# The learned message layer of a graph network: units transposed beforehand, tiles multiplied in pairs, all sums on TensorE

## The reference

```python
def _forward(x, edge_src, edge_dst, edge_vec, emb, norm, W1, W2):      # M = 8, MUL = 16, MOUT = 8
    xs = concat([x[edge_src, :8], x[edge_dst, :8]], axis=1)
    xv = concat([x[edge_src, 8:].reshape(E, 8, 3), x[edge_dst, 8:].reshape(E, 8, 3)], axis=1)
    h = 2.0 ** 0.5 * relu(emb @ W1 / 10.0 ** 0.5)                      # [E, 16]
    w = (h @ W2 / 16.0 ** 0.5).reshape(E, 7, MUL, MOUT)                # W2 is [16, 896]
    s_out = PW_S * (einsum('eu,euw->ew', xs, wa_s) + INV_SQRT3 * einsum('eui,ei,euw->ew', xv, y1, wb_s))
    g_out = PW_S * (einsum('eu,euw->ew', xs, wa_g) + INV_SQRT3 * einsum('eui,ei,euw->ew', xv, y1, wb_g))
    v_out = PW_V * (INV_SQRT3 * einsum('eu,ek,euw->ewk', xs, y1, wc) + INV_SQRT3 * einsum('eui,euw->ewi', xv, wd)
                    + einsum('eui,ea,iak,euw->ewk', xv, y2, W3J121, we))
    edge_ftr = concat([GAIN * tanh(s_out), (GAIN * tanh(g_out)[:, :, None] * v_out).reshape(E, 24)], axis=1) * norm
    return segment_sum(edge_ftr, edge_dst)
```

## Time and profile before

| | us |
|---|---|
| median of 3 runs | 16380.43 (16376.54 to 16397.94) |
| span of the profiled execution | 13418.0 |
| time of the profiled execution beside its span | not given by the page |
| PE busy | 6021.0 (45%) |
| PE weight loads busy | 5074.6 (38%) |
| DVE busy | 5448.5 (41%) |
| ACT busy | 2111.0 (16%) |
| POOL busy | 7502.6 (56%) |
| mean granted TensorE clock | 0.718 |

### The profile page before, as it was taken

One profiled execution on the slowest core, in us unless ns is written; L12 is line 12 of the kernel. 1 busy time (PEld: TensorE's weight loads), 2 busy tenths in 40 slices (PEclk: granted clock), 3 DMA queues, 4 the chain that ended last, 5 costly groups with the idle time before them and its releaser, 6 DMA issues. The chain is left out here.

```text
span 13418.0 us, 195196 instructions
## 1 busy us (share of the span) xinstructions
PE 6021.0 (45%) x81668; PEld 5074.6 (38%) x81668; DVE 5448.5 (41%) x7142; ACT 2111.0 (16%) x2759; POOL 7502.6 (56%) x7346
## 2 busy tenths in 40 slices
PE   1000000300000599999980000000399999999779
PEld 0000000300000599888970000000266666666578
DVE  4454555900000201111112233323488888888711
ACT  1111111000000000000001122111244444444300
POOL 5777776777777413030207777776655555555150
PEclk6555555555555799999985555555699999999889
DMA  4445453000000599889952111111111111111179
GB/s 173 165 168 189 163 175 122 0 0 0 0 0 0 208 368 358 327 310 343 363 209 42 39 42 42 39 39 23 25 32 32 32 32 32 32 32 33 36 271 340
DMA packets 516083, 1622.37 MB, mean 121 GB/s; under 512 B 233432, under 2 KB 315536, under 8 KB 424144
## 3 DMA queue, kind: packets, MB, share of 16 engines
q1 hardware_dynamic: 258272, 1346.21, 27.0%
q0 software_dynamic: 234368, 154.18, 6.1%
q10 hardware_dynamic: 22640, 110.04, 2.1%
HBM read 1262.48 MB, written 352.41 MB: 120 GB/s over the span
## 5 line engine op out<-in xcount | busy, mean ns | idle before, releaser
L197 POOL DMA_INDIRECT z_l<-table,idx_l x1568 | 1752.6, 1118 | 1234.2 <-DMA dir_p<-unit 739.5
L197 POOL DMA_INDIRECT g_l<-table_l,idx_l x1568 | 1649.2, 1052 | 511.0 <-issue 500.9
L843 POOL DMA_INDIRECT adj<-worth,sq x1568 | 1546.1, 986 | 545.7 <-issue 509.5
L1935 PE MATMUL p_r<-prod_k,ident 128*128 128x256 f32 x6272 | 1705.7, 396 | 239.4 <-DVE prod_k L2199 207.7
L197 POOL DMA_INDIRECT g_gat<-table,idx_gat x1568 | 1479.4, 944 | 514.0 <-issue 499.6
L1935 PEld LDWEIGHTS p_r<-prod_k,ident 128*128 128x128 f32 x6272 | 1132.9, 194 | 425.4 <-DVE prod_k L2199 274.7
L2199 DVE TENSOR_TENSOR prod_k<-p_t,h_l 128x512 f32<-128x512 f32 x1568 | 1071.1, 683 | 0.0
L999 PE MATMUL p_h<-wd,emb_s 80*128 80x128 f32 x392 | 104.2, 444 | 2009.1 <-ACT hid L1053 1847.5
L1567 PE MATMUL pr<-diag,ones 128*128 128x256 f32 x2 | 1.2, 714 | 2110.4 <-DVE diag L1585 2110.4
L407 PE MATMUL pc_l<-spread,cross_lo 128*128 128x448 f32 x28 | 25.3, 1023 | 1853.8 <-DVE spread L411 1690.4
L999 PEld LDWEIGHTS p_h<-wd,emb_s 80*128 80x128 f32 x392 | 87.8, 327 | 2025.4 <-ACT hid L1053 1855.8
(11 more groups left out here) (489 smaller groups left out, 13729.9 us busy)
## 6 DMA issues: line engine op xcount, KB each, us to landing
cells_cheb<-adj SPq DMA_DIRECT2D x560, 1344.0 KB
adj<-zeros SPq DMA_DIRECT2D x28, 7056.0 KB, 26.0
cells_l<-adj SPq DMA_DIRECT2D x140, 1344.0 KB
cells_cheb<-adj SPq DMA_DIRECT2D x56, 672.0 KB
gat_rows<-prod_gat ACTq DMA_DIRECT2D x28, 952.0 KB, 3.8
g_l<-table_l,idx_l POOLq DMA_INDIRECT x1568
start_rows<-zeros SPq DMA_DIRECT2D x28, 896.0 KB, 4.2
scanned_rows<-msg_l ACTq DMA_DIRECT2D x28, 896.0 KB, 9.7
```

What stands on the lines that cost most here:

```text
L197: return pool.indirect_dma_start(out=dest, out_offset=None, in_=table_ap, in_offset=bass.IndirectOffsetOnAxis(ap=index, axis=0))
L843: pool.indirect_dma_start(out=adj, out_offset=bass.IndirectOffsetOnAxis(ap=cell[:, t:t + 1], axis=0), in_=worth_u[:, t:t + 1], in_offset=N ...
L1935: last = nc.tensor.matmul(p_r[:].rearrange("p a k w -> p (a k w)"), ident[:], prod_k[q % 2][:, :, :, k:k + 2, :].rearrange("p g t k w -> p ...
```

## The change

The weights of layer 2 and the transposed hidden units are made once, in layer 0. `w_terms` [128, 384] f16 holds the scalar weights in four 32-row bands (high and low part, for the high and the low part of the features), `w_vec` [128, 128] bf16 the vector weights. They are scaled by a power of two found with a maximum over partitions (one more PE matmul); `w_unit` undoes it in tanh and gate. `hidden_t` holds for every edge the 16 hidden units, in 128 rows of bf16 parts, with the edges in columns: after the scatter's one-hot work PE computes emb @ W1 in 224 blocks of 896 edges, ACT takes the relu in bf16, DVE the rest, ACT copies it to two bands of 32 partitions, DVE subtracts again in one band, SP stores the block. Eight more copies of W1 are loaded at the start of SP's program, behind `wd`, and 40 pieces of W2 after the keys are made; some 45 small DVE operations make the weights after the one-hot loop.

The two DVE copies in the attention's norm stage go; scatter and table take `x_cur`. The first block of layer 2 goes; its one gather stands at the head of POOL's program in the main block.

In the main block zs is 64 columns wide, zv is gone. PE transposes zs twice a tile, into partitions 0 to 63 and 64 to 127. Per tile one f16 product of 384 columns (features against `w_terms`: column (k, group, w)) and one bf16 product of 128 columns (`hidden_t` of the tile against `w_vec`: column (u, w)) remain; p_t has room for three pairs of tiles. DVE's `pair` takes two tiles in two operations of 768 elements: the scalar groups from PSUM times the hidden units, the vector weights from PSUM times the features xv. Both write `prod` [4 tiles, 16, 48], of which there are three. All six groups are summed on PE, 16 f32 matmuls of 192 columns a quad; ACT copies the one sum of 192 columns out. The DVE reduction, the addition of halves, `odd` and p_r go. SP loads `hidden_t` in two parts of 28 tiles a chunk. PE issues the products of a quad one quad ahead, transposes two ahead. ACT's `take` copies z to `zsf` and `xv` when all 56 gathers of the chunk have landed; `high`, `leave` and `low` are one operation each of 1792 elements. The core of the diff:

```diff
+        hidden_t = nc.dram_tensor("hidden_t", [P, T * P], BF16).ap()
...
+        w_terms = keep("w_terms", [P, 3 * 16 * M], F16)
+        w_vec = keep("w_vec", [P, 16 * M], BF16)
+        w_unit = keep("w_unit", [P, 2])
+        ident_h = keep("ident_h", [P, P], F16)
...
+                HB = 896
+                HALF_B = HB // 2
+                n_ht = T * P // HB // 2
+                assert 2 * n_ht * HB == T * P and HALF_B <= 512 and 5 * HB <= CH * 112
+                emb_q = [flat_rows[0][0:10, b * HB:(b + 1) * HB] for b in range(2)]
+                parts_q = [flat_rows[0][:, 2 * HB + b * HALF_B:2 * HB + (b + 1) * HALF_B].bitcast(BF16) for b in range(2)]
+                rest_q = [flat_rows[0][:, (3 + b) * HB:(4 + b) * HB] for b in range(2)]
+                parts_h = [a.rearrange("p (h n) -> p h n", h=2) for a in parts_q]
+                rest_h = [a.rearrange("p (h n) -> p h n", h=2) for a in rest_q]
...
+                            for k in range(8):
+                                sp.dma_start(w1r[:, 16 * k:16 * k + 16], w1).then_inc(w1r_in, 16)
...
+                        def load_emb(k, b):
+                            sp.dma_start(emb_q[b], emb_t[:, bass.ds(k * HB, HB)]).then_inc(emb_in[b], 16)
+
+                        def store_parts(k, b):
+                            sp.wait_ge(ht_third, k + 1)
+                            sp.dma_start(hidden_t[:, bass.ds(k * HB, HB)], parts_q[b]).then_inc(ht_out[b], 16)
+                        for b in range(2):
+                            sp.sem_inc(ht_out[b], 16)
+                            load_emb(b, b)
+                        with sp.Fori(0, n_ht - 1) as i:
+                            for b in range(2):
+                                store_parts(2 * i + b, b)
+                                load_emb(2 * i + b + 2, b)
+                        for b in range(2):
...
+                        with v.Fori(0, n_ht) as i:
+                            for b in range(2):
+                                k = 2 * i + b
+                                v.wait_ge(ht_first, k + 1)
+                                V.scalar_tensor_tensor(rest_h[b], pre_h[b], 0.0, parts_h[b], ALU.max, ALU.subtract).then_inc(ht_rest, 1)
+                                v.wait_ge(ht_second, k + 1)
+                                V.tensor_tensor(parts_q[b][96:P, :], rest_q[b][96:P, :], parts_q[b][96:P, :], ALU.subtract).then_inc(ht_third, 1)
...
+                        with pe.Fori(0, n_ht) as i:
+                            for b in range(2):
+                                k = 2 * i + b
+                                pe.wait_ge(emb_in[b], 16 * (i + 1))
+                                pe.wait_ge(ht_rest, k + 1)
+                                for h in range(2):
+                                    last = nc.tensor.matmul(pre_h[b][:, h, :], w1r, emb_q[b][:, h * HALF_B:(h + 1) * HALF_B],
+                                                            start=True, stop=True)
+                                last.then_inc(ht_made, 1)
...
+                        with act.Fori(0, n_ht) as i:
+                            for b in range(2):
+                                k = 2 * i + b
+                                act.wait_ge(ht_made, k + 1)
+                                act.wait_ge(ht_out[b], 16 * (i + 1))
+                                A_.activation(parts_h[b], pre_h[b], ACT.Relu).then_inc(ht_first, 1)
+                                act.wait_ge(ht_rest, k + 3)
+                                A_.activation(parts_q[b][32:64, :], rest_q[b][32:64, :], ACT.Copy)
...
-                            V.tensor_copy(sq[:, js, 0:M], x_cur[:, js, 0:M])
-                            V.tensor_copy(sq[:, js, M:D].rearrange("p j (i m) -> p j m i", i=3),
-                                          x_cur[:, js, M:D].rearrange("p j (m i) -> p j m i", i=3)).then_inc(s_vdone, 1)
+                            v.sem_inc(s_vdone, 1)
...
+                prod = [sb(f"prod{k}", [P, 4, 16, COLS]) for k in range(3)]
...
+                def scalar_part(k, t):
+                    return p_t[:, k * 1024 + t * 640:k * 1024 + t * 640 + 384]
+
+                def scalar_pair(k):
+                    return p_t[:, k * 1024:k * 1024 + 1280].rearrange("p (t f) -> p t f", t=2)[:, :, 0:384]
+
+                def vector_part(k, t):
+                    return p_t[:, k * 1024 + 384 + t * P:k * 1024 + 384 + (t + 1) * P]
+
+                def vector_pair(k):
+                    return p_t[:, k * 1024 + 384:k * 1024 + 640]
...
+                def pair_buffer(b, pr):
+                    return (pr + b) % 3
+
+                def prod_buffer(b, q):
+                    return q % 3 if b == 0 else (1 if q == Q - 1 else (q + 2) % 3)
...
+                        def load_hidden(c, k):
+                            sp.dma_start(h_t[k][:], hidden_t[:, bass.ds((c * 2 + k) * HT * P, HT * P)]).then_inc(ht_in[k], 16)
...
+                        row_gather(pool, fill[:], table, first_row[:]).then_inc(s_agg, 16)
...
-                        def transposes(c, b, q):
...
+                        def transposes(b, q):
+
                             for t in range(4):
+                                for half in range(2):
+                                    last = nc.tensor.transpose(p_z[64 * half:64 * half + 64, t * P:(t + 1) * P], zs[b][:, 4 * q + t, :], ident_h[:])
...
+                        def products(c, b, q, half, first=False):
+
+                            pr = 2 * q + half
+                            back = lag(pair_buffer, b, pr, PRS)
+                            if half == 0:
+                                pe.wait_ge(zt_ready, c * Q + q + 1)
+                            if not first or pr >= back:
+                                pe.wait_ge(t_used, c * PRS + pr - back + 1)
+                            if pr % (HT // 2) == 0:
+                                pe.wait_ge(ht_in[2 * pr // HT], 16 * c + 16)
+                            k = pair_buffer(b, pr)
+                            for t in range(2):
+                                tile = 2 * half + t
+                                place = (2 * pr + t) % HT
+                                h_of = h_t[(2 * pr + t) // HT]
+                                nc.tensor.matmul(scalar_part(k, t), zt[q % 2][:, tile * P:(tile + 1) * P], w_terms[:], start=True, stop=True)
+                                last = nc.tensor.matmul(vector_part(k, t), h_of[:, place * P:(place + 1) * P], w_vec[:], start=True, stop=True)
...
+                            for k in range(4 * part, 4 * part + 4):
+                                last = nc.tensor.matmul(p_sum_out, ident[:], prod[prod_buffer(b, q)][:, :, k, :],
+                                                        start=(k == 0), stop=(k == 15))
...
+                                next_products(0)
+                                if q + 2 < Q:
+                                    transposes(b, q + 2)
+                                elif more:
+                                    transposes(other, q + 2 - Q)
+                                last_sums(0)
+                                last_sums(1)
+                                next_products(1)
+                                last_sums(2)
+                                last_sums(3)
...
+                        def summed(c, b, q):
+                            act.wait_ge(red_made, c * Q + q + 1)
+                            A.activation(out6[b][:, :, :, 4 * q:4 * q + 4].rearrange("p g w t -> p t (g w)"),
+                                         p_sum_out.rearrange("p (t f) -> p t f", t=4), ACT.Copy).then_inc(red_out, 1)
...
+                        def take(c, b, times, first=False):
+
+                            act.wait_ge(gathered[b], 16 * CH * (times + 1))
+                            if not first:
+                                act.wait_ge(t_used, (c - 1) * PRS)
+                            A.activation(zsf[:, :, 0:M], z[b][:, :, 0:M], ACT.Copy)
+                            A.activation(xv[b][:, :, 0:24], z[b][:, :, M:D], ACT.Copy).then_inc(z_taken, 1)
...
+                        def high(c, b):
+                            act.wait_ge(p_done, c + 1)
+                            A.activation(zs[b][:, :, 0:32], zsf[:], ACT.Copy).then_inc(h_split, 1)
+
+                        def low(c, b):
+                            act.wait_ge(d_done, c + 1)
+                            A.activation(zs[b][:, :, 32:64], zsf[:], ACT.Copy, scale=LOW).then_inc(z_split, 1)
...
+                        def pair(c, b, pr, first=False):
+                            q, half = pr // 2, pr % 2
+                            k = pair_buffer(b, pr)
+                            tiles = slice(2 * pr, 2 * pr + 2)
+                            back = lag(prod_buffer, b, q, Q)
+                            v.wait_ge(t_made, c * PRS + pr + 1)
+                            if half == 0 and (not first or q >= back):
+                                v.wait_ge(red_made, c * Q + q - back + 1)
```

(53 more changed lines are left out.)

596 lines of the change are left out of this document (243 added, 353 removed).

## The result

The changed kernel took 16646.7 us (median of 4, 16591.9 to 16703.8) where the kernel before took 16378.7: ratio 1.0163, 95% interval 1.0137 to 1.0188, slower by 1.6%. The prediction said 15868, some 3% faster. Its profiled execution took 16635.6 us with a span of 16633.9: here nothing lies around the span but 1.7 us, and in every other run whose span is on record it is 1.7 to 2.6 us, so that, other than said ahead of the prediction, the device time holds next to nothing beside the span. The 2962 us that I had put "around the span" of the kernel before were therefore suspect first of all.

A forecast was written before the change was run, and what follows sets the result against it. PE was taken as first bound of the learned layer, DVE second. Learned layer -515 and start DMAs +3, new loop hidden, made -512: span 12906 plus 2962 held fixed, time 15868, range of 8 in 10 from 15730 to 16200.

The forecast's parts named there:

- so 2962 us lie around the span, which I hold fixed: Whole kernel: median 16380.4 against profiled span 13418.0; the 2962 us between stay unchanged, so span 12906 gives time 15868.
- It costs nothing until then and 224 us for each us above: New loop in the first layer: free up to 7.24 us a block, beyond that 224 us for each us.
- The cover of 1622 us: First layer: the scatter's stretch from 2745 on, 1622 us, hides the new loop of 1280 to 1340 us.
- rival (4): First layer: the new loop outlasts the scatter; 16870 if its two buffers do not overlap at all; chance 0.06.
- Rival (2): Learned layer: a pass can't start faster than one weight load, 0.194 us; +410 us, time 16278; chance 0.03.
- the case of unhidden loads: Learned layer: no weight load hides behind a pass; +87 us a chunk, +2400, time 18280; chance 0.02.
- Rival (1): Learned layer: the waits between DVE and PE stay; 96 to 106.4 us a chunk, time 15951 to 16239; chance 0.22.
- my case: Learned layer: a chunk takes 90.7 to 96 us, time 15805 to 15951; chance 0.58.
- rival (5): The part around the span shrinks with it, 15755; second half: a tile's two transposes run side by side, 15783; chance 0.05.
- my -512: Whole kernel: -515 us in the learned layer plus 3 us for eight more DMAs at the start.

The follow-up runs named there:

- e14: The changed kernel with POOL's adjacency scatter held back until the counting loop is done, against the kernel before: 15873.5 us against 16412.6, ratio 0.9672.
- e4: The changed kernel with POOL's adjacency scatter held back until the counting loop is done, against the kernel before: 13479.1 us against 13399.3, ratio 1.0056.
- e5: The kernel before with POOL's adjacency scatter held back until the counting loop is done, against the kernel before: 13797.9 us against 13399.3, ratio 1.0288.
- e8: The changed kernel with no edit, run again and profiled, against the kernel before: 13067.3 us against 13411.0, ratio 0.9738.
- e1: The kernel before with no edit, profiled again, against the kernel before: 16382.6 us against 16381.4, span 16380.8.

## Why the prediction was wrong

The step that failed is the last of the sum: "so 2962 us lie around the span, which I hold fixed". There was no such part. Profile and runs came from chips of two kinds, and on the kind that was timed, the 2962 us lay inside the kernel, where PE gets on slowly while POOL issues DMAs. The times stood 22% above the span, which should have told me that the profile was not of the execution to be predicted, and I gave only rivals that scaled the rest. The step that fell with it, and that turned a gain into a loss: "It costs nothing until then and 224 us for each us above". The cover of 1622 us supposed the counting done by 2745; on chip A half of it is done when the scatter ends, so there is no cover at all, and the loop that I had put at nothing costs 1274. My rival (4) had the right place and mechanism, the loop on the path, with 0.06; but I priced it by a slower block, not by a cover that goes.

On chip A the sum is, from the spans: first layer +1279 (next stage at 4715 and 5994), learned layer -1020 (5011 and 3991, last scatter before to first gather after), where -515 was forecast, the rest -6, together +253, which is the difference of the spans. On chip B,' kind, profile against profile:

- Learned layer: forecast -515, measured -403 (3283 to 2880). The chunk was forecast at 93.0; behind the first ones it took 97.1 in the mean (before 110.4), by turns 93.4 and some 100.7. The 112 missing are this: 27.7 chunks of 4.1 are 114. PE's own work, a chunk without waits, is 93.4 where I had summed 90.7. The rest lies in every second chunk: DVE's side jobs between pairs, 50.9 us of waits in some 26 chunks, 2 each, and the stretches at half clock behind them.
- Pass of 192 columns: 0.161 forecast, start to start 0.162 with loads of 0.19 beside them. Rival (2) and the case of unhidden loads are out. Rival (1) has the right size, since 97.1 lies in its 96 to 106.4 and not in my case's 90.7 to 96, but not by its reasons: of 15.7 us of old waits 2 were left, and DVE's operations took 953 and 947 ns, forecast 946.
- Transposes: rival (5)'s second half was right. The two of a tile, in different halves of the array's columns, start 3 to 4 ns apart, and the next pair 53 ns later, so a pair costs one. What this saves is more than spent on gaps between groups, which my sum had at nothing: sixteen passes take 2.65 to 2.70, not 2.58, and before and behind the transposes PE starts nothing for some 0.1 us each.
- New loop: 5.7 to 6.0 us a block forecast, 5.88 beside the scatter on chip B, 5.61 alone on chip A, but 11.0 beside the scatter on chip A (e14). But not free where covered: +66 (next stage at 4374 and 4440), 70 in the pair e4, e5. POOL's DMAs slow a little beside it; I had put this at nothing.
- Eight DMAs at the start: +3 forecast. The first gather came at 122.5 to 125.6 in the five profiles without them and at 125.1 to 128.4 in the thirteen with them, 3 us apart in the mean.
- What I said would prove me wrong did: loop after the scatter, layer over 2850, and median minus span not 2962.

Put on chip B's time, my -512 would have been 13411 - 512 = 12899 against 13067: right in direction, with 2.6% where 3.8% were forecast.

## What to carry to other kernels

Where the profile's span and the runs' time differ by more than a few us (2.6 was the most in these runs), take the profile to be of another kind of execution: ask for one whose span fits before building a sum on it, and treat no remainder as fixed. Work that is to hide behind a long stretch of POOL's indirect DMAs should be counted in instructions of PE, not in us: on some chips PE gets one in 1.40 us there, so a loop of many small matmuls (28 instructions of PE for 3.4 us of DVE) must not lie there, and a loop of 8 large ones may. Cover is used up in order: before new work is put behind it, check that the work already there ends in time on the slowest kind of chip.

## What the runs showed of the hardware

- Chips differ: the same kernel took some 13400 us on four and 16379 to 16413 on three of the sets, with nearly identical busy times of DVE and ACT in the learned layer (2641 and 2645, 1343 and 1344). What makes a chip one kind or the other stays open, and so does whether it is the fetching of PE's instructions: the profile calls it `issue` and no more, and the late updates of semaphores (`remote`) would not be explained by it.
- On chip A, the hold-ups of PE that were looked at stand beside POOL's indirect DMAs: the counting took 405 us with POOL silent (e14), and in 2172 us beside the scatter 127 of its 252 DVE instructions got done (e1). Loads of SP at 357 GB/s did not hold PE up: 1000 matmuls took 46 us beside them and 118 beside 56 of POOL's DMAs.
- Transposes of 64 columns of the array, two into its two halves, start 3 to 4 ns apart, and the next two 53 ns later (e8).
- f32 passes of 192 columns start 0.162 us apart though a weight load of 0.19 belongs to each. By the Trainium skill ("TensorE: Matmul & The Clock Gate", section "What overlaps and what doesn't") such a load would not be hidden; by that rule the trace disagrees here too.
